# A graph network on one NeuronCore: part of the edge-attribute products goes from VectorE to TensorE and ScalarE, and the zeroing of a table moves one stage later

## The reference, cut to what matters

```python
concat_z = jnp.concatenate([z[edge_src], z[edge_dst], w], axis=-1)   # w: edge_attr_64, 100000 x 64
e = jax.nn.leaky_relu(concat_z @ W_att.T, negative_slope=NEG_SLOPE)[:, 0]
```

## Time and profile before

| | |
|---|---|
| median of 3 runs | 8701.62 us (8699.66 to 8706.0) |
| the profiled execution | 8684.55 us, span 8682.8 us |
| counting stage | 27.8 to 321.8 us of the span |
| first projection | 385.5 to about 801 us |
| busy over the span | PE 69%, DVE 63%, POOL 61%, ACT 36% |
| mean granted TensorE clock | 0.833 |

### The profile page before, as it was taken

One profiled execution on the slowest core, in us unless ns is written; L12 is line 12 of the kernel. 1 busy time (PEld: TensorE's weight loads), 2 busy tenths in 40 slices (PEclk: granted clock), 3 DMA queues, 4 the chain that ended last, 5 costly groups with the idle time before them and its releaser, 6 DMA issues. The chain is left out here.

```text
span 8682.8 us, 115466 instructions
## 1 busy us (share of the span) xinstructions
PE 5971.4 (69%) x29150; PEld 4478.0 (52%) x29150; DVE 5445.1 (63%) x14404; ACT 3085.7 (36%) x9088; POOL 5264.1 (61%) x5183
## 2 busy tenths in 40 slices
PE   0266777876379755566599999975477775574599
PEld 0133555554367433344477777764355553453487
DVE  8787888887766566665544444446577767445444
ACT  0111888888522200000233333322244444222322
POOL 0274666664667677777677777755777771434422
PEclk9688999998589877777599999977788886786699
DMA  9412666665266433333111111116333343563364
GB/s 303 156 51 75 174 175 171 171 174 145 81 185 202 146 92 101 101 101 102 34 28 31 27 30 31 27 18 183 103 104 103 105 101 117 164 211 87 118 201 162
DMA packets 634189, 1018.39 MB, mean 117 GB/s; under 512 B 135674, under 2 KB 437378, under 8 KB 633356
## 3 DMA queue, kind: packets, MB, share of 16 engines
q0 software_dynamic: 243360, 540.20, 23.8%
q1 hardware_dynamic: 364508, 418.40, 15.2%
q10 hardware_dynamic: 25744, 53.10, 2.1%
HBM read 793.35 MB, written 225.75 MB: 117 GB/s over the span
## 5 line engine op out<-in xcount | busy, mean ns | idle before, releaser
L4182 POOL DMA_INDIRECT gat_edges_rows<-gat_table,gat_room x1080 | 1167.4, 1081 | 339.0 <-issue 326.4
L2759 POOL DMA_INDIRECT l_edges_ring<-pairs,first_room x832 | 842.2, 1012 | 525.6 <-issue 242.7
L2321 POOL DMA_INDIRECT l_sum_rows<-l_feats,back_room x832 | 828.1, 995 | 265.7 <-issue 244.9
L2341 PE MATMUL l_sum_o<-l_sum_rows,l_sum_s 128*128 128x256 f32 x1664 | 615.1, 531 | 459.0 <-DVE l_sum_s L2352 215.1
L2810 ACT ACTIVATE l_edges_ring<-l_edges_ring,l_edges_weight 128x64 f32<-128x64 f32 x3328 | 816.6, 336 | 0.0
L2341 PEld LDWEIGHTS l_sum_o<-l_sum_rows,l_sum_s 128*128 128x128 f32 x1664 | 414.9, 263 | 653.7 <-DVE l_sum_s L2352 318.0
L2882 PE MATMUL l_edges_o<-l_edges_ring,l_edges_sf 128*128 128x260 f32 x1664 | 533.7, 426 | 144.8 <-DVE l_acc L3015 137.3
L3803 ACT ACTIVATE m_ffn_ht<-m_ffn_hp,m_ffn_b1t 128x256 f32<-128x256 f32 x592 | 280.1, 473 | 872.7 <-PE m_ffn_hp L3771 872.7
L2363 DVE TENSOR_TENSOR l_acc<-l_acc,l_sum_o 128x256 f32 x832 | 349.8, 420 | 357.0 <-PE l_sum_o L2341 269.4
L3781 PE MATMUL m_ffn_yp<-m_ffn_w2b,m_ffn_ht 128*128 128x256 f32 x2368 | 547.8, 385 | 27.7 <-ACT m_ffn_ht L3803 27.1
L3771 PE MATMUL m_ffn_hp<-m_ffn_xt,m_ffn_w1b 128*128 128x256 f32 x2368 | 548.8, 385 | 6.1 <-DVE m_ffn_xt L3818 3.4
(11 more groups left out here) (862 smaller groups left out, 14675.5 us busy)
## 6 DMA issues: line engine op xcount, KB each, us to landing
sorted_rows<-count_main_zero ACTq DMA_DIRECT2D x1, 51858.0 KB, 237.0
m_ffn_xs<-sorted_rows SPq DMA_DIRECT2D x144, 258.0 KB, 3.5
m_ffn_w1b<-in_L_ffn_w SPq DMA_DIRECT2D x32, 1024.0 KB, 5.7
m_ffn_w2b<-in_L_ffn_w SPq DMA_DIRECT2D x32, 1024.0 KB, 5.4
m_ffn_w1b<-in_L_ffn_W SPq DMA_DIRECT2D x56, 512.0 KB
m_ffn_w2b<-in_L_ffn_W SPq DMA_DIRECT2D x56, 512.0 KB
m_by_node<-gat_edges_ys SPq DMA_DIRECT2D x96, 256.0 KB
count_main_attr<-in_edge_attr SPq DMA_DIRECT2D x34, 644.0 KB
```

Of the source, the lines that this page charges most:

```text
L2321: pool.indirect_dma_start(rows[:, slot, j, :], None, table, bass.IndirectOffsetOnAxis(ap=L.src[:, t:t + 1], axis=0)).then_inc(got[slot], 16)
L2341: pe.matmul(o[:, j, 0:D], s4[:, q % S4, j, :], rows[:, slot, j, :], start=True, stop=True).then_inc(out_done, 1)
L2759: pool.indirect_dma_start(rows(q, 0, 2 * D)[:, j, :], None, table, bass.IndirectOffsetOnAxis(ap=L.src[:, t:t + 1], axis=0)).then_inc(got[q ...
L4182: pool.indirect_dma_start(rows[:, slot, j, :], None, table, bass.IndirectOffsetOnAxis(ap=L.src[:, q * B + j:q * B + j + 1], axis=0)).then_ ...
```

## The change

Of the 782 columns 306 leave VectorE: nine units of 34 columns (`UNITS`, `UC`). SyncE loads a unit to `attr_u`, two buffers. TensorE takes it in 17 blocks of 128 values (two edges of 64 attributes on each partition), transposes a block against the identity (`turn`), ScalarE copies up to four transposed blocks from PSUM at once (a batch; 45 batches), and TensorE multiplies each block, as stationary operand, with `w2` of 128 x 2 (`dot`), where column k holds the weights in rows 64k to 64k+63. All 306 sums stay in one PSUM bank until ScalarE copies them to `ew`. The other 476 columns stay on VectorE as 28 shares of 17 columns, 14 in each loop. The unit loads are threaded between the first 14 share loads. The column sums (`tot`, 1) stand behind all units on TensorE.

The zeroing leaves `count_edges`. In the first projection VectorE clears a tile `zero` first of all, and SyncE adds to each of the 49 steps a DMA of 4 or 5 times 128 x 516 floats (`wipe`), in the queue of the stores and behind that step's store.

```diff
@@ count_edges @@
+        late_banks = ph.ps("late_banks", [P, 3, 512])
+        blk, flips, dots = late_banks[0:1], late_banks[:, 0:2, :], late_banks[:, 2, :]
-        AC = 23 if attr_d is not None else 0
-        AB = 4
+        AC, AB, UC, UNITS, BATCH = 17, 4, 34, 9, 4
+        NA = (C - UNITS * UC) // AC
+        blocks = UC // 2
+        batches = [(u, b, min(b + BATCH, blocks)) for u in range(UNITS) for b in range(0, blocks, BATCH)]
...
+                sp.wait_ge(gone, 1)
+                for k in range(2):
+                    sp.dma_start(w2[k * 64:(k + 1) * 64, k:k + 1], weights.rearrange("o k -> k o")).then_inc(attr_in, 16)
+
+                def load_unit(u):
+                    c0 = NA * AC + u * UC
+                    if u >= 2:
+                        sp.wait_ge(flipped, (u - 1) * per_unit)
...
+                half = NA // 2
+                for q in range(half):
+                    for u in range(q * UNITS // half, (q + 1) * UNITS // half):
+                        load_unit(u)
+                    load_share(q)
+                for q in range(half, NA):
+                    load_share(q)
...
-                @block.scalar
-                def _(act):
-                    act.wait_ge(filled, 2)
-                    act.dma_start(clear.rearrange("(p r k) d -> p r (k d)", p=P, k=2),
-                                  bc(zero[:], 1, [P, clear.shape[0] // (2 * P), 2 * ROW])).then_inc(placed, 16)
+            @block.scalar
+            def _(act):
+                for i, (u, lo, hi) in enumerate(batches):
+                    act.wait_ge(flipped, i + 1)
+                    if i >= 2:
+                        act.wait_ge(dotted, i - 1)
+                    act.copy(turned_attr[:, i % 2, 0:(hi - lo) * P], flips[:, i % 2, 0:(hi - lo) * P]).then_inc(carried, 1)
+                act.wait_ge(dotted, len(batches))
+                act.wait_ge(gone, 2)
+                act.copy(ew[:, NA * AC:C], dots[:, 0:UNITS * UC]).then_inc(carried, 1)
...
-                            add_share(k * 22 // T)
+                        add_share(k * (NA // 2) // T)
...
-                        add_share(22 + (k + 1) * (NA - 22) // T)
+                    add_share(NA // 2 + (k + 1) * (NA - NA // 2) // T)
...
+                def turn(i):
+                    u, lo, hi = batches[i]
+                    if lo == 0:
+                        pe.wait_ge(unit_sem[u % 2], 16 * parts_in * (u // 2 + 1))
+                    if i >= 2:
+                        pe.wait_ge(carried, i - 1)
+                    for b in range(lo, hi):
+                        ins = pe.transpose(flips[:, i % 2, (b - lo) * P:(b - lo + 1) * P],
+                                           attr_u[:, u % 2, b * P:(b + 1) * P], core.ident[:])
+                    ins.then_inc(flipped, 1)
+
+                def dot(i):
+                    u, lo, hi = batches[i]
+                    pe.wait_ge(carried, i + 1)
+                    for b in range(lo, hi):
+                        c0 = u * UC + 2 * b
+                        ins = pe.matmul(dots[:, c0:c0 + 2], turned_attr[:, i % 2, (b - lo) * P:(b - lo + 1) * P], w2[:],
+                                        start=True, stop=True)
+                    ins.then_inc(dotted, 1)
+                pe.wait_ge(attr_in, 48)
+                turn(0)
+                for i in range(len(batches)):
+                    if i + 1 < len(batches):
+                        turn(i + 1)
+                    dot(i)
                 pe.wait_ge(tot, 1)
@@ project @@
+                if clear is not None:
+                    sp.wait_ge(zeroed, 1)
+                    cleared_rows = clear.rearrange("(p r k) d -> p r (k d)", p=P, k=2)
+                    times = clear.shape[0] // (2 * P)
+
+                    def wipe(t, par):
+                        lo, hi = t * times // T, (t + 1) * times // T
+                        sp.dma_start(cleared_rows[:, lo:hi, :], bc(zero[:], 1, [P, hi - lo, 2 * ROW])).then_inc(cleared, 16)
+                    stages.append((late, wipe))
```

More of the change, by code:

```diff
@@ L348, in count_edges @@
     with Phase(nc, f"count_{L.name}") as ph:
-        carrier = Carrier(nc, ph, beside) if beside else None
         cq = -(-C // Q)
@@ L357, in count_edges @@
         rl = ph.sb("rl", [P, W])
-        ew = ph.sb("ew", [P, W]) if attr_d is not None else None
+        ew = ph.sb("ew", [P, W])
         out = ph.sb("out", [P, L.quads, 5 * Q], I32)
@@ L421, in _ @@
                                      .rearrange("(o c) -> o c", o=1)).then_inc(listed, 16)
[L422 to L433, removed]
-                                     ).then_inc(att_sem[par], 16)
+                weights = watt_d[0:1, 2 * D:2 * D + 64]
@@ new lines, in load_share @@
+                def load_share(q):
+                    par = q % AB
+                    if q >= AB:
+                        sp.wait_ge(scored, q - AB + 1)
+                    for lo, hi in shares:
+                        sp.dma_start(attr[lo:hi, par], attr_v[lo:hi, q * AC:(q + 1) * AC, :]
+                                     ).then_inc(att_sem[par], 16)
+                    sp.dma_start(attr[full:full + 1, par], attr_t[:, q * AC:(q + 1) * AC, :]
+                                 ).then_inc(att_sem[par], 16)
@@ L470, in _ @@
                 done(dve.memset(rl[:], 0.0))
-                if ew is not None:
-                    done(dve.memset(ew[:], 0.0))
+                dve.memset(w2[:], 0.0).then_inc(gone, 1)
+                dve.memset(ew[:], 0.0).then_inc(gone, 1)
                 done(dve.memset(fill[:], 0))
@@ L495, in _ @@
                 shares_added = [0]
-                if attr_d is not None:
-                    dve.wait_ge(attr_in, 16)
+                dve.wait_ge(attr_in, 48)
+                dve.wait_ge(gone, 2)
                 def add_share(upto):
@@ L1772, in project @@
         sorter = also(ph) if also else None
+        zero = ph.sb("zero", [P, 2 * ROW]) if clear is not None else None
+        zeroed, cleared = ph.sem("zeroed"), ph.sem("cleared")
         assert front or follow or sorter
@@ L1860, in _ @@
                     follow.landed(sp)
+                if clear is not None:
+                    sp.wait_ge(cleared, 16 * T)
                 if park is not None:
@@ L1953, in _ @@
             def _(dve):
+                if clear is not None:
+                    dve.memset(zero[:], 0.0).then_inc(zeroed, 1)
                 if front:
@@ L3104, in layer0_gnn @@
                         (skip, "out", 3 * D, 4 * D, 0)],
-                to_sbuf=[(core.x, 0)], beside=unmoved.take(MOVES[2]),
+                to_sbuf=[(core.x, 0)], beside=unmoved.take(MOVES[2]), clear=core.sorted_rows,
                 also=lambda ph: also(ph, const))
```

53 lines of the change are left out of this document (26 added, 27 removed).

## The result

| | before | after |
|---|---|---|
| median of 3 runs | 8701.62 us (8699.66 to 8706.0) | 8648.07 us (8647.69 to 8659.91) |
| the profiled execution | 8684.55 us, span 8682.8 | 8659.91 us, span 8657.7 |
| counting stage ends | 321.8 us | 279.5 us |
| the stage behind the first projection (`l_edges`) begins | 801.8 us | 759.9 us |
| busy over the span | PE 69%, DVE 63%, POOL 61%, ACT 36% | PE 70%, DVE 62%, POOL 61%, ACT 36% |

The ratio of the medians is 0.994, 95% interval 0.9923 to 0.9958: 54 us less, between 37 and 67. The forecast was 8662, so the change was faster as forecast, by 14 us more than I said, and 2 us past the fast end of the forecast's own range (8650 to 8676).

The account below looks back on a forecast made before the run. VectorE's instruction stream was taken to bound the counting stage. Terms -42.1 - 0.5 + 2 + 1.5 gave -39 us, so 8701.6 became 8662, with bounds of 8654 to 8676, or 8650 to 8676 with the spread of runs.

Parts of the forecast that it names:

- VectorE's shares, minus 42.1 and 0.5 of preparations: Counting stage: 34 shares become 28 shorter ones, minus 42.1 us; zero memset and hand-overs leave, minus 0.5.
- TensorE's 153 blocks, nothing: Counting stage: TensorE's 50 or 99 us of blocks stay hidden before VectorE asks for the sums, cost nothing.
- the rival of a late TensorE: First counting loop: low clock and exposed hand-overs make VectorE wait 12 to 18 us, gain 24, 8678; chance 0.08.
- Loads, nothing: First counting loop: 20 MB in 110 us, 180 GB/s against 320 shown, so loads cost nothing.
- Second loop, nothing: Counting stage's second loop: VectorE's turn of 1.74 or 1.64 us stays above TensorE's 1.34 a bucket; nothing.
- the rival of the low clock there: Second counting loop: clock stays low, 131 us against VectorE's 81, plus 50, total 8712; chance 0.02.
- The wipes, plus 2: First projection: zeroing DMAs delay the last stores, plus 2 us, ends 0 and 8.
- the rival of 0.04: First projection: wipes far slower than 4.8 us set the tiles' pace; at 9.6, 176 us added, 8840; chance 0.04.
- the rival that the projection gives 10 to 20 us back: First projection: wipes stretch GpSimd's scatters or the tail's steps by 10 to 20 us, 8675 to 8680; chance 0.07.
- Semaphores, plus 1.5: The sum has a term of plus 1.5 us that the prediction's text as given does not explain.
- The sum, minus 39: Whole kernel: -42.1 - 0.5 + 2 + 1.5 gives -39 us, bounds -48 to -26, median 8662.
- if a stage behind the projection moves: Sign for the stages after the first projection: if one moves, the prediction is wrong; no size given.

Follow-up runs that it names:

- a wide matmul: The change plus a 512-column bf16 matmul of constants, result unused, behind each batch's dots: 10694.99 us in one execution, stage end 279.2.
- the second chip: Chip of the first four follow-up kernels, where the kernel before takes 10797 us; the unedited change measured 10744.12 there, ratio 0.9957.
- the third comparison: The unedited change again, against the kernel before on a chip where that takes 8704.64 us: 8665.36 us, ratio 0.9956, stage end 278.9.
- the split alone: The change with the zeroing left on ScalarE's queue in the counting stage: 10773.02 us, ratio 0.9973 to the kernel before, stage end 298.2.
- the kernel of thirteen units with wide matmuls: The change with 13 units, 20 shares on VectorE and a 512-column matmul per batch: 10722.61 us, ratio 0.9952 to the kernel before, stage end 275.7.

## Why the prediction was right, and where it was off

*VectorE's shares, minus 42.1 and 0.5 of preparations.* Right. At `cnt` 38.5 us are won (said 37.6 and 0.5), and from there to the last share 4.6 (said 4.4), 43.1 in all where I said 42.6. A pass takes 1.285 us (said 1.29), so the slope between 784 and 1472 elements holds. That the absent zeros gain nothing by themselves is shown by the kernel that only moves them: 0.6 us in the stage. VectorE's stream sets the stage's end as long as the zeros are elsewhere; with them in place it was their landing.

*TensorE's 153 blocks, nothing.* Right, and by the branch that I had as the worse one: the clock stayed at 1.2 GHz throughout, the last dot came at 139 (said 144), and 14 us were to spare (said 10). A batch took 2.45 us, said 2.6. ScalarE's copies and the hand-overs do not show between batches (TensorE is busy all of the 93.50 us), so the rival of a late TensorE, which needed the low clock and those hand-overs, had its first half and not its second. (Its own sum was off too: 13.5 us a unit from 42 on end nine at 163 to 164, not at 165 to 171.) The Trainium skill, "TensorE: Matmul & The Clock Gate", section "Part 4: PE-mode transpose", with its rule that the full clock does not engage for transposes, fits this stretch (transposes at 1.2 GHz from 46 to 139 us), but not the second of the earlier trace rows, nor the four in 0.60 us with a wide matmul among them.

*Loads, nothing.* Right: 165 GB/s in the first loop (said 180), and VectorE waits for none. What I did not see is that with the zeros left in place the loads would not have bound either; the landing of the zeros would, at 295, and the stage would have ended at 298.

*Second loop, nothing.* Right: a bucket takes VectorE 1.61 us ((238.4 - 159.3) / 49; said 1.64 to 1.74), and the place matmuls rose to the full clock as before, 515 ns in the mean, so the rival of the low clock there did not come.

*The wipes, plus 2.* At the upper edge or too high: 0.1 us from the first store to the last in the two profiles of the result, 1 to 2 us on the second chip, and two profiles of the change itself differ by 1.2 there (352.3, 353.5). I had a backlog over the three gaps of the tail. The gaps are as before, 9.80 us for three. The last wipe is issued at 748.24, ahead of the last store but one, and none stands between that store and the last. All that shows of a backlog is that SyncE took 0.81 and 1.26 us to issue two `skip` stores there instead of 0.43, and nobody waited for it. That wipes set the pace fell with the same 352.29 us, and so did the rival that the projection gives 10 to 20 us back.

The prices behind this term were misread. I took 237 us for the zeros and 36.4 for the fill from the earlier trace rows; both count up one semaphore, and the profile gave the zeros' end to the fill. By the traffic of the queues before, the fill was through by 272, within 17 us of its issue, and the zeros' last packets ran at 291, 256 us after theirs: 5.2 us a wipe, not 4.8, and no sign of a slow queue, on which I had built the rival of 0.04.

*Semaphores, plus 1.5.* The counting stage's six cost at most 0.8 (9.32 where the earlier trace rows has 8.57), the first projection's two 0.3 (5.99 against 5.70). Eight projections at 0.3 and the 0.8 would be 3.2 by this estimate, just above my 0 to 3; over the rest of the program the drift hides it.

*The sum, minus 39.* At the end of the first projection it is minus 42.0, where my terms give -42.1 - 0.5 + 2 and some 0.6 of clears, -40.0; the missing 2 are the wipes, and VectorE's extra 0.5 pays for clears that cost more than I said. The bounds were added up wrongly: my own best ends (44.2 and 1, with nothing lost) give -45 and not -48, and 0.7 of the slope gives 35.3 for the shares and not 37. By my terms the range was 8656 to 8677, and the measured 8648 lies 8 below it.

*The median*, 8648, is 14 under the forecast. Of this only the 2 us of the wipes are a mistake that the runs show. Three comparisons give 54, 53 and 39 us with intervals of 37 to 67, 31 to 62 and 27 to 50, and 42 lies in all three. So the mechanism was right and the direction safe, but how near the first median came to the forecast was up to the drift: the third comparison, by 39 us, hits it.

My list of signs called it wrong "if a stage behind the projection moves". That sign was a poor one: stages move between two profiles of the same kernel. The change's first and third profile stand at 760.6 and 762.0 behind the projection, 2123.2 and 2131.2 at the first mixture, 3061.6 and 3067.5 at `l_sum_o`, 5847.7 and 5848.3 at `l_turn`, 8650.6 and 8648.7 at the end, up to 8 us apart. On the second chip the change and the kernel that only moves the zeros, alike behind the counting stage, stand 42.4 us apart at its end, 53.0 at the first mixture, 22.2 at `l_turn` and 53.5 at the end; there the drift is up to 20 us. The "few us" that I allowed for repeated runs were too few.

Whether the change moves a later stage by a few us stays open. From the first mixture to `l_sum_o` the lead over the other kernel shrank in each pair of profiles, by 6.7 us in the first, 4.6 with the change's third profile (against the same one of before) and 2.8 on the second chip. That is one direction, but no fixed size, within what the same kernel drifts.

## What to carry to other kernels

- When work goes to an engine that stands idle, compute when it ends at the low clock and compare this with the moment the bound engine asks; here a unit adds 10.3 us to TensorE and brings VectorE's request 2.5 forward, so a margin of 14.1 says that one more unit fits, with 1.3 left (measured 1.5 and 1.8), and four more don't.
- A wait in a shared DMA-issuing program passes lateness on to every load behind it. Thirteen units starved VectorE of its shares (27.6 us), well before it came to the sums (6.8).
- Where background transfers fill a stage to the brim, shortening the computation alone moves the end to their landing. Move them to a stage with room, and judge both edits together: at the stage's end the move of the zeros alone gave 0.6 us, the split alone 23.6, both together 42.3.
- Where two DMAs count up one semaphore, the profile's landing times can be given to the wrong one. Read the traffic by queue before a price is taken from them.

## What the runs showed of the hardware

- TensorE stayed at 1.2 GHz for 93.5 us in which it was busy without a gap, with transposes (0.27 us apiece) and matmuls of two columns (0.21 a record), while the clock column of that stretch says 1.00. The length of single records, four transposes in 1.06 or 0.60 us, tells which clock it was. The column did not, up to its first change: in the kernel of thirteen units with wide matmuls it says 1.00 for 60 to 100 us, where every wide matmul takes 0.59.
- The zeros on their own queue, with the DMA engines full (1.04), made no load late that VectorE needed; they came last themselves. The 1664 KB of fill were through within 17 us beside them (before, by the traffic of its queue; the 36.4 of the earlier trace rows ends with the zeros' landing) and landed in 7.3 in the change:

```profile
main_records<-count_main_fill SPq DMA_DIRECT2D x1, 1664.0 KB, 7.3
```
